# A factorization-machine kernel: 24 end chunks in eight pieces instead of 32 in nine, a fifth single group, and a new order of work in the end

## The reference

```python
x_reg = input_data @ W_lin.T + b_lin
emb = input_data @ factors
sum_squared = jnp.square(emb.sum(axis=1))
squared_sum = (jnp.square(input_data) @ jnp.square(factors)).sum(axis=1)
h = jax.nn.relu(emb @ W1.T + b1)
h = jax.nn.relu(h @ W2.T + b2)
dnn_out = h @ W3.T + b3
x = x_reg + 0.5 * (sum_squared - squared_sum)[:, None] + dnn_out
x = 0.5 + jax.nn.sigmoid(x) * 5.0
```

## Time and profile before

| | |
|---|---|
| median of three runs | 133.76 us (133.70 to 133.83) |
| the profiled execution's own time | 133.76 us |
| its span (first to last instruction) | 132.0 us |
| granted TensorE clock, mean | 0.974; 1.00 in every stretch read from 86 us on |
| TensorE busy | 107.0 us (81%) |
| ScalarE busy, VectorE busy | 61.5 us (47%), 52.6 us (40%) |
| the loads' queue | 52.23 MB, 93.2% of 16 engines' span |
| chain that ended last | DMA 54%, TensorE 40% of the span |

### The profile page before, as it was taken

The page is one execution under the profiler, slowest core; times in us unless marked ns, Lnnn a source line. Parts: engine busy times, 40 slices in busy tenths (PEclk is TensorE's granted clock), DMA queues, the critical chain, the costliest instruction groups (busy, mean ns, idle before and its releaser), DMA issues.

```text
span 132.0 us, 2607 instructions
## 1 busy us (share of the span) xinstructions
PE 107.0 (81%) x1123; PEld 34.6 (26%) x1123; DVE 52.6 (40%) x51; ACT 61.5 (47%) x52; POOL 15.7 (12%) x48
## 2 busy tenths in 40 slices
PE   6099969429979839749749979999998987989992
PEld 4012222002212112112112233322222112345881
DVE  0391063027036036046045016565351351576571
ACT  4030067029039039049048046868562561465851
POOL 3015000200010200200200110164530000000000
PEclk9999999995999999999977999999999999999999
DMA  3999899989999998998999999899999999999700
GB/s 106 413 531 417 377 477 472 407 387 467 427 387 462 457 427 387 457 437 387 467 457 427 387 457 447 377 432 412 452 407 407 462 415 417 418 404 411 302 26 1
DMA packets 3489, 52.36 MB, mean 397 GB/s; under 512 B 404, under 2 KB 536, under 8 KB 1560
## 3 DMA queue, kind: packets, MB, share of 16 engines
q1 hardware_dynamic: 3480, 52.23, 93.2%
HBM read 52.22 MB, written 0.00 MB: 396 GB/s over the span
## 4 chain that ended last, share of the span: by engine, by line
DMA 54%; PE 40%; SPq 2%; DVE 1%; issue 1%; ACT 1%
DMA xr<-in_x_pairs 43%; PE p_lin L506 34%; DMA xr<-in_x_end 11%; PE p_sq L506 2%; PE p_h L601 2%; SPq L273 1%; PE p_tot L506 1%; PE p_h L632 1%; PE p_tot L614 0%; DVE h L454 0%; DVE h L449 0%; SPq L267 0%; SPq L266 0%; PE p_tot L621 0%; SPq L265 0%
## 5 line engine op out<-in xcount | busy, mean ns | idle before, releaser
L327 ACT ACTIVATE sq<-xr 128x2560 f32<-128x2560 f32 x20 | 45.9, 2333 | 46.8 <-DMA xr<-in_x_pairs 38.8
L427 DVE TENSOR_TENSOR sq<-xr 128x1536 f32<-128x1536 f32 x20 | 34.6, 1761 | 53.7 <-DMA xr<-in_x_pairs 42.9
L506 PE MATMUL p_lin<-xr,wr 128*17 128x512 f32 x320 | 39.9, 638 | 15.6 <-DMA xr<-in_x_pairs 14.4
L506 PE MATMUL p_lin<-sq,wz 128*18 128x512 f32 x320 | 37.7, 592 | 0.0
L506 PEld LDWEIGHTS p_lin<-xr,wr 128*17 128x17 f32 x320 | 9.2, 102 | 44.5 <-issue 38.4
L307 POOL COPY wr<-hd 128x136 f32 (+1 forms) x20 | 9.3, 464 | 75.0 <-PE p_lin L506 75.0
L506 PEld LDWEIGHTS p_lin<-sq,wz 128*18 128x18 f32 x320 | 10.1, 98 | 25.8 <-issue 25.0
L506 PE MATMUL p_lin<-xr,hd 128*17 128x352 f32 (+1 forms) x128 | 10.0, 380 | 1.3 <-DMA xr<-in_x_end 1.3
L437 DVE TENSOR_TENSOR sq<-xr 128x1408 f32<-128x1408 f32 (+3 forms) x6 | 6.6, 1135 | 6.1 <-DMA xr<-in_x_end 6.1
L337 ACT ACTIVATE sq<-xr 128x1408 f32<-128x1408 f32 (+3 forms) x6 | 5.7, 983 | 6.3 <-DMA xr<-in_x_end 6.3
L506 PE MATMUL p_lin<-sq,ws 128*18 128x352 f32 x64 | 6.6, 459 | 0.0
(11 more groups left out here) (52 smaller groups left out, 40.8 us busy)
## 6 DMA issues: line engine op xcount, KB each, us to landing
xr<-in_x_pairs SPq DMA_DIRECT2D x8, 4096.0 KB, 21.9
xr<-in_x_groups SPq DMA_DIRECT2D x4, 2048.0 KB, 18.3
xr<-in_x_end SPq DMA_DIRECT2D x1, 2112.0 KB, 10.5
xr<-in_x_end SPq DMA_DIRECT2D x3, 640.0 KB, 12.0
xr<-in_x_end SPq DMA_DIRECT2D x1, 1760.0 KB, 14.3
xr<-in_x_end SPq DMA_DIRECT2D x1, 1056.0 KB, 12.4
hd<-in_head SPq DMA_DIRECT2D x1, 952.0 KB, 4.8
xr<-in_x_end SPq DMA_DIRECT2D x1, 704.0 KB, 13.7
```

What stands on the lines that cost most here:

```text
L327: nc.scalar.activation(sq[:, ring(s), BY_DVE:CHUNKS, :], xr[:, s, BY_DVE:CHUNKS, :], ACT.Square).then_inc(act_squared, 1)
L427: nc.vector.tensor_tensor(sq[:, ring(s), 0:BY_DVE, :], xr[:, s, 0:BY_DVE, :], xr[:, s, 0:BY_DVE, :], ALU.mult).then_inc(dve_squared, 1)
L506: return nc.tensor.matmul(out, lhsT, rhs, start=False, stop=False, skip_group_check=True)
```

## The change

`ENDS` goes from 32 to 24. The eight chunks that leave the end become a fifth single group (group 20), 512 columns wide; `TOTAL` becomes 21 and `END_SLOT` 3. Block 1 now ends in pieces of 8, 6, 6 and 4 chunks, and block 2 in pieces of 8, 8, 6 and 2. SP's wait before a piece loses the term `END_SLOT`. Each engine's order in the end is new: ScalarE's squares are no longer in the order of the pieces, so `act_count` looks them up in `ACT_ORDER`.

```diff
-ENDS = 32
+ENDS = 24
...
-PIECES = ((1, 0, (4, 2), (4, 2)), (1, 12, (4, 1), (4, 1)), (1, 22, (3,), (3,)), (1, 28, (2,), (2,)),
-          (2, 0, (2, 2), (2, 2)), (2, 8, (2, 2), (2, 2)), (2, 16, (2, 2), (2, 2)), (2, 24, (2, 1), (2, 1)),
-          (2, 30, (1,), (1,)))
+PIECES = ((1, 0, (4,), (4,)), (1, 8, (3,), (3,)), (1, 14, (3,), (3,)), (1, 20, (2,), (2,)),
+          (2, 0, (2, 2), (2, 2)), (2, 8, (2, 2), (2, 2)), (2, 16, (2, 1), (2, 1)), (2, 22, (1,), (1,)))
+
+ACT_ORDER = ((0, 0), (1, 0), (2, 0), (3, 0), (4, 0), (4, 1), (5, 0), (6, 0), (7, 0), (5, 1), (6, 1))
...
-            return sum(len(q[2]) for q in PIECES[:i]) + j + 1
+            return ACT_ORDER.index((i, j)) + 1
...
-                sp.wait_ge(sq_used, RING + TOTAL - SLOTS + END_SLOT + last_slot(i) + 1)
+                sp.wait_ge(sq_used, RING + TOTAL - SLOTS + last_slot(i) + 1)
...
@@ ScalarE @@
-            square_end(0, 0)
-            square_end(0, 1)
-            square_end(1, 0)
-            square_end(1, 1)
+            square_end(0)
+            square_end(1)
             square_end(2)
             square_end(3)
             square_end(4, 0)
             act.wait_ge(p_lin_done[1], 1)
             copy_lin(1, 0)
             copy_lin(1, 1)
+            square_end(4, 1)
             nc.scalar.copy(rest[:, :], p_lin[1][:, BLOCKS[1][1]:HALF]).then_inc(rest_copied, 1)
-            embedding_square(1)
-            square_end(4, 1)
             layer1(1, BLOCKS[1][1])
             square_end(5, 0)
+            square_end(6, 0)
+            embedding_square(1)
+            square_end(7)
             square_end(5, 1)
-            square_end(6, 0)
             square_end(6, 1)
-            square_end(7, 0)
-            square_end(7, 1)
-            square_end(8)
-            sigmoid(1)
             embedding_square(2)
             act.wait_ge(squares_done, 1)
             nc.scalar.copy(qs[:, :], p_sq[:, 0:BLOCKS[LAST][1]]).then_inc(qs_ready, 1)
+            sigmoid(1)
             sigmoid(2)
@@ VectorE, after square_end(6, 0) @@
-            layer2(1)
             square_end(6, 1)
-            square_end(7, 0)
-            square_end(7, 1)
             dve.wait_ge(rest_copied, 1)
             copy_block(2)
-            square_end(8)
-            scale(1)
+            square_end(7)
+            layer2(1)
             dve.wait_ge(p_h1_done[2], 1)
             layer1(2, p_h1[1], BLOCKS[2][1])
             layer2(2)
+            scale(1)
             scale(2)
@@ TensorE, from block 1's end on @@
             pe.wait_ge(lin_ready[1], 2)
-            embedding_sum(1)
 
             pe.wait_ge(h1a_ready[0], 1)
             first_layer(p_h1[0], BLOCKS[1][1], lin[:, cols(1)]).then_inc(p_h1_done[1], 1)
-            linear(1)
-            embedding_square(1)
+            act_squares_end(4, 1)
             multiply_end(5)
             dve_squares_end(5, 0)
+            embedding_sum(1)
             pe.wait_ge(h1a_ready[1], 1)
             layer2(1)
-            act_squares_end(4, 1)
             multiply_end(6)
+            multiply_end(7).then_inc(p_lin_done[2], 1)
+            dve_squares_end(5, 1)
+            dve_squares_end(6, 0)
             act_squares_end(5, 0)
-            dve_squares_end(5, 1)
-            act_squares_end(5, 1)
-            multiply_end(7)
-            multiply_end(8).then_inc(p_lin_done[2], 1)
-            layer3(1)
-            add_squares_end(6)
+            act_squares_end(6, 0)
+            linear(1)
             pe.wait_ge(lin_ready[2], 1)
 
             pe.wait_ge(h1b_ready[0], 1)
             first_layer(p_h1[1], BLOCKS[2][1], lin[:, cols(2)]).then_inc(p_h1_done[2], 1)
-            add_squares_end(7)
+            dve_squares_end(7)
+            dve_squares_end(6, 1)
+            act_squares_end(7)
 
             pe.wait_ge(sg_ready[0], 1)
             embedding_sum(2)
-            add_squares_end(8).then_inc(squares_done, 1)
+            act_squares_end(5, 1)
+            act_squares_end(6, 1).then_inc(squares_done, 1)
+            embedding_square(1)
+            layer3(1)
             pe.wait_ge(h1b_ready[2], 1)
             layer2(2)
             linear(2)
```

## The result

| | before | after |
|---|---|---|
| median (five runs each, same chip) | 133.83 us (133.70 to 133.97) | 134.60 us (134.48 to 134.63) |
| ratio to before, 95% interval | | 1.0055 (1.0043 to 1.0067) |
| span of the profiled execution | 132.0 us | 132.7 us |
| scale of block 2 ends | 130.00 | 130.79 |

The account below looks back on a forecast made before the run. Bound taken: last landing plus the chain of block 2's dense layers, TensorE's other work just hidden. Landing 0.00, TensorE's backlog +0.12, rest of the way to layer 2 +0.23: +0.35 us, 133.76 to 134.11; range 133.65 to 134.6.

Parts of the forecast that it names:

- The upper bound: Whole time: 16 small matmuls at 0.54 instead of 0.30, stores in each other's way for 0.25: +0.84, 134.60 us.
- Landings: Loads of the end: block 1 is loaded 1.5 us later, the last landing stays at 126.38, SP's wait costs nothing: 0.00.
- Late engines catch up: Rival, end of the loads: the new cut evens the DMA engines, landings up to 1.2 us earlier, 132.9; chance 0.11.
- a late engine gets later: Rival, last landing: an instruction packet falls on an already late DMA engine and delays it by 1.2, 135.3; chance 0.07.
- TensorE's backlog up to block 2's sum: TensorE before block 2's copy: multiply 6 starts 0.2 late, sum complete at 127.04 for 126.92, +0.12.
- In between TensorE makes 16 squares' matmuls and `linear(1)`, 0.69 ... hidden with 0.1 to spare: Between block 2's sum and first layer: this work ends at 127.43, before the first layer starts at 127.54.
- TensorE stands until 127.98: After block 2's first layer: TensorE, free at 127.82, waits for VectorE's square of piece 7, made from 127.60 to 127.93.
- Then 12 matmuls of squares (0.41): Ahead of block 2's layer 2: these, embedding sum (0.07) and 16 small matmuls (0.30) free TensorE at 128.76, 0.35 later.
- the old chain from layer 2's start on: From block 2's layer 2 to the end: steps as before, `scale(2)` ending at 130.35.
- The 16 small matmuls: `embedding_square(1)` and `layer3(1)` ahead of block 2's layer 2: 0.30, or 0.40 by the skill's rule, giving 134.21.
- The stores: End, on SP: the two stores' transfers follow by 0.7 us instead of 2.1; between 0 and 0.5, taken as 0.
- the work stays hidden: Rival, block 2's layer 2: VectorE's relu sets its start, 128.58, +0.17 or less, 133.9, no difference; chance 0.27.

Follow-up runs that it names:

- e3: The kernel after with `embedding_square(1)` and `layer3(1)`, 16 small matmuls, moved behind block 2's layer 2: 134.51 us, 1.0054 to the kernel before.
- e6: The kernel after with block 2's squares on the four groups in turn and the small matmuls behind layer 2: 134.27 us, 1.0027 to the kernel before.

## Why the prediction was right in kind and half in size

That the time still lies at 134.6, the edge of the range, is luck. The upper bound was made of dearer small matmuls (0.24) and of stores in each other's way (0.25). Neither happened in the kernel after: the small matmuls cost no more than their price, and the last store left when its scale was done. What filled the gap, the groups, stood in no term.

- **Landings: right.** The seven whose squares ScalarE starts at the landing (106.54 to 123.28) were within 0.03 us, the next two within 0.05, and the dropped term in SP's wait was free, as the run with it alone shows. "Late engines catch up" and "a late engine gets later" did not happen.
- **TensorE's backlog up to block 2's sum: right.** Forecast +0.12, measured +0.16 (copy at 127.20).
- **"In between TensorE makes 16 squares' matmuls and `linear(1)`, 0.69 ... hidden with 0.1 to spare": this step failed.** It priced them by the chain's 0.54/16, which is eight chunks in a row on four groups. In the order of the change the first layer started 0.22 later than forecast (0.04 of it from the copy), and was then torn apart as well: its last result came 0.31 later than forecast. In turn on the groups it came at 128.13.
- **"TensorE stands until 127.98" for the square of piece 7: wrong, without effect.** That square was done at 127.76 (VectorE began it 0.24 behind the copy and not 0.44), while the first layer still occupied TensorE. Nor did `layer2(1)` on VectorE push block 2's relu to 128.15: it was over at 128.07, and the relu waited for the first layer until 128.42.
- **"Then 12 matmuls of squares (0.41)" and the old chain from layer 2's start on: the same failure again.** Three of the six chunks lie on one group, and layer 2 needs all four: it started 0.20 later than forecast and took 0.59 for 0.35. Of the 0.79 at the last scale, 0.35 was forecast. The other 0.44 is what the copy-to-relu stretch loses when the squares go to the groups in turn and nothing else is changed (2.40 to 1.96). The mechanism of the forecast, TensorE's uncovered work ahead of layer 2, was right; its term was mis-sized, since it counted matmuls and not the fullest group's.
- **The 16 small matmuls: right.** Moved away, they gave 0.28 at layer 2's relu, for 0.30; with the squares in turn, 0.18. The Trainium skill's rule of 25 ns from start to start (TensorE: Matmul & The Clock Gate, "Wait — 56ns, not 53.3ns?") gives an estimate of 0.40 for them; the trace of the kernel before stays below it, at 19 ns, on four groups side by side.
- **The stores: the bound held, the value taken was right for this kernel.** In the two kernels with the small matmuls behind layer 2, block 1's store does delay the last one: by 0.22 in e3 (0.76 for 0.54) and by 0.24 in e6 (0.77 for 0.53).
- **The rival "the work stays hidden"** rested on a better overlap of those matmuls. The overlap was worse.

That matmuls to different groups run side by side is also what the Trainium skill says (TensorEngine Tiling (Array Packing), "Key Properties": tiles work independently, and each is tied to its own PSUM partitions). The trace agrees with that. The page does not say what an uneven order costs; the runs on two groups do.

## What to carry to other kernels

Where small matmuls are packed on groups of the array, cost a stretch by its fullest group, not by the count of matmuls: write down the group of each one in the order of issue, before and after a reorder. When sums are accumulated anyway and a final step adds the groups up, the group need not follow from the data's index, and dealing them out in the order of issue added no instruction here and took 0.3 us off. And a step that gets later because it is "off the path" may still share a queue with the last one: here two stores on SP.

## What was not expected of the hardware

- A price read from a dense row can be a fourth of what one instruction occupies: 0.034 us per matmul in the earlier trace rows, and 0.136 us on one group. With two of the four groups, the same number of matmuls made the kernel before 1.7 us longer.
- Matmuls on different groups did not start in the order of the program: in the rows after, a `p_sq` matmul starts at 127.61, though `linear(1)`, which stands behind all of them, began at 127.49 (L615), and layer 2's last one starts 0.36 us behind its first.
- An issue of a store of 1.4 KB holds SP for 0.5 us, and so does the one of 0.6 KB behind it.
